# A two-layer decoder on one core: the units of four chains laid in a new order on every engine

## The reference, cut to what matters

```python
x = _layernorm(x + _L0_attn_ref(x, ...))         # selective scan (16 states, 512 channels), conv, gate
x = _layernorm(x + _L0_xattn_ref(x, ctx_768, ...))  # cosine similarities of x and a context
x = _layernorm(x + _L0_ffn_ref(x, ...))          # top 2 of 4 experts, 1024 hidden
x = _layernorm(x + _L1_attn_ref(x, ...))         # 16 heads of 64, softmax over 256 keys
x = _layernorm(x + _L1_xattn_ref(x, ctx_768, ...))  # softmax attention to the context
x = _layernorm(x + _L1_ffn_ref(x, ...))          # state c: batch b needs the state after batch b-1
...
def step(h, inp):                 # of the scan: for each channel and state, along the 256 tokens
    dAt, dBxt, Ct = inp
    h = dAt * h + dBxt
    y = jnp.einsum('bdn,bn->bd', h, Ct)
    return (h, y)
```

## Time and profile before

| | |
|---|---|
| time, median of 3 runs | 1320.05 us (1315.18 to 1323.99) |
| profiled execution, first to last instruction | 1318.1 us |
| mean granted TensorE clock (1 is 2.4 GHz) | 0.953 |
| busy: PE / DVE / ACT / POOL | 1170.0 / 1038.5 / 792.2 / 199.2 us |
| instructions | 16965 |

### The profile page before, as it was taken

One profiled execution on the slowest core, in us unless ns is written; L12 is line 12 of the kernel. 1 busy time (PEld: TensorE's weight loads), 2 busy tenths in 40 slices (PEclk: granted clock), 3 DMA queues, 4 the chain that ended last, 5 costly groups with the idle time before them and its releaser, 6 DMA issues.

```text
span 1318.1 us, 16965 instructions
## 1 busy us (share of the span) xinstructions
PE 1170.0 (89%) x6026; PEld 905.1 (69%) x6026; DVE 1038.5 (79%) x1642; ACT 792.2 (60%) x1978; POOL 199.2 (15%) x258
## 2 busy tenths in 40 slices
PE   5786778988988999999998999999999899999984
PEld 3554545766867767877787777877776767677763
DVE  3999799899878997999869998897959994434215
ACT  4334545378637874686657864875577545646624
POOL 0100020111322212121212121111111211010002
PEclk7888879989999999999999999999999989999998
DMA  5611010223231343233322333322232311000211
GB/s 212 205 44 47 34 54 19 72 63 79 37 96 33 84 86 100 53 65 64 81 72 61 66 56 96 82 51 41 63 87 65 80 33 45 1 1 9 64 63 64
DMA packets 41190, 86.67 MB, mean 66 GB/s; under 512 B 3737, under 2 KB 14970, under 8 KB 40466
## 3 DMA queue, kind: packets, MB, share of 16 engines
q1 hardware_dynamic: 27282, 60.42, 14.4%
q0 software_dynamic: 13824, 25.17, 11.0%
HBM read 54.38 MB, written 6.04 MB: 46 GB/s over the span
## 4 chain that ended last, share of the span: by engine, by line
PE 55%; DVE 25%; ACT 10%; issue 5%; DMA 2%; POOL 2%; ACTq 0%; DVEq 0%; SPq 0%; POOLq 0%
PE bank L295 18%; DVE scans L555 7%; PE bank L510 5%; PE bank L1194 5%; PE bank L1174 4%; DVE scans L560 4%; DVE scans L551 3%; PE bank L906 3%; PE bank L1225 3%; PE bank L900 3%; PE bank L712 3%; ACT scans L531 2%; PE bank L1183 2%; DMA scans<-scans 2%; DVE conv L433 2%
## 5 line engine op out<-in xcount | busy, mean ns | idle before, releaser
L555 DVE TENSOR_TENSOR_SCAN scans<-scans 128x1024 f32<-128x1024 f32 x128 | 292.4, 2284 | 15.3 <-ACT scans L531 8.0
L531 ACT ACTIVATE scans<-dt,a_neg 128x255 f32<-128x255 f32 x512 | 220.7, 502 | 0.0
L510 PE MATMUL bank<-scans,ident 128*128 128x256 f32 x640 | 180.7, 418 | 29.1 <-DVE scans L560 20.2
L510 PEld LDWEIGHTS bank<-scans,ident 128*128 128x128 f32 x640 | 125.0, 206 | 67.2 <-DVE scans L560 26.3
L588 POOL DMA_DIRECT2D scans<-scans x96 | 84.5, 880 | 512.4 <-DVE scans L560 512.2
L560 DVE TENSOR_TENSOR scans<-scans,BC 128x1024 f32<-128x1024 f32 x128 | 155.8, 1217 | 1.3
L551 DVE TENSOR_TENSOR scans<-conv,BC 128x1024 f32<-128x1024 f32 x128 | 155.5, 1215 | 0.1
L1194 PEld LDWEIGHTS bank<-v,ya 128*128 128x128 f32 x1024 | 122.6, 192 | 21.5 <-issue 20.4
L1194 PE MATMUL bank<-v,ya 128*128 128x65 f32 x1024 | 128.5, 276 | 1.8 <-ACT yo L1257 1.6
L1265 ACT ACTIVATE ya<-bank,nmax 128x256 f32<-128x256 f32 x256 | 100.7, 482 | 43.7 <-DVE nmax L1332 43.5
L1332 DVE TENSOR_REDUCE nmax<-bank 128x2 f32<-128x512 f32 x128 | 82.0, 682 | 45.2 <-PE bank L1174 44.8
(11 more groups left out here) (264 smaller groups left out, 2063.8 us busy)
## 6 DMA issues: line engine op xcount, KB each, us to landing
BC<-xpj_scratch SPq DMA_DIRECT2D x31, 1024.0 KB, 5.9
scans<-scans POOLq DMA_DIRECT2D x96, 256.0 KB, 3.3
xin<-in_x SPq DMA_DIRECT2D x8, 256.0 KB, 2.8
conv<-in_x SPq DMA_DIRECT2D x8, 256.0 KB, 2.8
out<-scans SPq DMA_DIRECT2D x8, 256.0 KB, 2.1
kept_x<-x SPq DMA_DIRECT2D x7, 256.0 KB, 2.0
kept_w<-wa SPq DMA_DIRECT2D x7, 256.0 KB, 2.0
BC<-kept_w SPq DMA_DIRECT2D x1, 1792.0 KB, 9.8
```

Source lines behind the costliest of these rows:

```text
L510: last = pe.matmul(sums_of(c), ident[:, :], step_of(b, u)[:, i, :], start=False, stop=(h == UH - 1 and i == SUMMED[b] - 1), skip_group_che ...
L531: ins = act.activation(step[:, j, 1:S], dt[b % 2][:, c, 1:S], ACT.Exp, scale=a_neg[:, c, n:n + 1])
L555: dve.tensor_tensor_scan(flat(H[:, :, :]), flat(H[:, :, :]), flat(dBx), 0.0, ALU.mult, ALU.add).then_inc(s["a_scan"], 1)
```

## The change: another `ORDER`

The five strings are replaced; every letter occurs as often as before, and no function is touched. The same instructions run with the same waits, in another order on each engine. Of the strings, the lines below are those from which places are counted in the text (a line holds 110 letters; PE's eighth line begins at place 770).

```diff
     "pe": (
-        "FFFFFFFWWWSSFFSSYYYFSYFYSYWYSYSYYYSYYSYYSYSFSSFSFSFFSSSFSFWWSWFSWSFSSWFSFWWSWFSWSWWSWWWSWWFSWFSWWWWSWWSWSWSSYS"
-        "YYYYYYYWWYYWYSYWYYYYSYYYYYWFYSYYYYWYYYYWYWSYYYSYYYYYWYYWSYYYWWYFSYWFYYYWYFSSYWWFYYWSYYWWYYSYYYYSWWWSWWFFSYYYYY"
...
-        "WWYWYFWYYYSYYWYYYSYYWYWWSYYYYWYYWWYWWYYWSWWSYWYWWSWWWWWSYYYYYSYWYWSSYYSYWYWSYWYYYSYWYWYYSWYWYWWWWWWSYSYSWSYYYY"
-        "YYWWYYWYYYWYYWYYYYYYYWYWWYYWYWWYWWYWYWWYYYWYWWYYYYYWWYYWYYWYYWYYYYYWWYYYYYYYWYYWYYWYYWWYYWYYYYYWYYYYYWYYYYYWYY"
-        "YYYWYYYYYWYYYYYWYYYYYWYYYYYYYYYYWWWWWWWWWWWWWWWWWWWWWWW"
+        "FFFFFFFFSFSSWWWFSFSYYFSSFFFSSYYSYFWYYYSYSYYYSYSSYYSSSSYWFFWWFSSWSWFSFFSFWWWSSSWWWSFWWFSWWSWWWWWWSWWWSSYSYYYWSY"
+        "YYYYYSYSSYYYWSWYYYYWYYSYWYYWYSYYYYYYYSYWYYWYYWYYFYYSYYSYYYYYWSWYYWYYSWYWYWYWYWYSWYWYYWWSWYYSWFWSFWFSYSYYYYWSWY"
...
+        "WYYWSYYWFYYYSYYWYYWYYYWSYYYWWYWYSWWYWYYWWSWYYWWSYWYWWSYYWYWYSYYYYWSYWSWYWYYYWYYWYSWYYWYWYSWWYSYWWYSYWYYWYYYSYY"
+        "YSWYYSYYSYYYYYWWWYYYWYWYYYYYYWYWYWYYWYWWYWWYYWYWWYWYYWWYWWYWWWYYYYYWWYYYYYWYYYYWYWYYYWWYYWYWYYYYWYYYYWYWYWYYYY"
+        "WYYYYWYYYYYYYYYWYYWYYYYYYYYYYYYYYYWWWWWWWWWWWWWWWWWWWWW"
     ),
     "act": (
-        "FFFFFFFFFSSSSSSFSSFFSSSSFFSSFSSWSSSSSSSSSSSSFFSSFSSFFFFFFSSSSSSSWFSSWFFSSFSSWFSSSSFSSFWWSSWFSSWSSWWSSWFWSSWFSS"
...
+        "FFFFFFFFFSSSFSSFFSSSFFSSSFSFSFFSSSFSFFSSSSWSSSSSSSSFSSSFSSSSFSWFWFSFSSFWSSFSFFSSFWSSWWSSWWSSSWFSFSWSWSSWSWWSWS"
...
     ),
     "dve": (
-        "FWWFFFFFSSWWSSWWSFSSWSFSSFSYSSYSYSSYSYSSYSYSSYSYSSYSYSSYSYSSYSYSSYSFSSSFSSFSFSSSSSSFSFSFFSSSSSSSSFSSSFSSFSFSSW"
-        "SSSSSSWSFSSFSWSSWSWSSFSFSSWSWSSSSSWSSSSWSSSSSSWSSWSSSSYYSYSSYSYSSYYSWFYYSSYSWYYYSSFYYSYWSSWYYSYWSYYSYFSFSSYYYS"
...
+        "FFFFFWWFSSSSFSSSFSWSSFSWSWSWSFSSWSFSSFSFSSYSYSSFSYSSFSYSSYSYSSYYSYSSYSYSSSYSSSSSSYSSFYSFSSYYSSSSFSSSFSWFSSFSWS"
+        "SFSFSSSFSSWSWSSWSFSSWSWSSSSSWSSSSWSSSSSWSWSSSSSYSYSYSYSYSSSYYSSSYYSSSYWSYYSYWYYSYFSYYSYSWSYSYSWYSYYSSWYSYYSSFY"
...
```

More of the change, by code:

```diff
@@ L64 @@
[L64 to L68, removed]
@@ L69 @@
-        "YWYYYYYWYYYYYWWYWWWWWWWWWWWWWWWWWWWWW"
+        "FFFFFFFFFSSSFSSFFSSSFFSSSFSFSFFSSSFSFFSSSSWSSSSSSSSFSSSFSSSSFSWFWFSFSSFWSSFSFFSSFWSSWWSSWWSSSWFSFSWSWSSWSWWSWS"
+        "SSSWYSWSYYYYYYYSSSYYSYYSSWYYSWYSYYWSYYSYYFYYYSYYWYWYYSYYYYSYWYYSFYYSYYYFYSWSWSYYWYFYYSSWYWYYWSSSYWYWSSSWSYFSSF"
+        "WSYSSWYFWYWWSWYYWYWWFWYWSSSFWYSSYYWSSWWYYSSFSYWSYWFYYWYYYWSYYYSFYYSYYWYYWYYSSYYSYSWYYYYYYYSYYFSFWSWYWYSWYYYWSS"
+        "WSYWWYSWSSYYSYSWSWSWYYFWWWSWYWYYWWFYWSSSYYSWSSSYWYYWYYWSSFYYSYYYSWWSYYSYWYYSFSYYWYYYSSYYWYYWYWYFYYYSWSYFWYWSYY"
@@ new lines @@
+        "YYWSFYWWYSSYWYYSSWFYWSYFFYSYFYSSSWWSWFSYWWYSWWWWYYYWYWFYWSSSYSSSYWSWYYWSYYSFYYWYWSYYWSYYFYYWYSSYYFYSYYSFYYWYYY"
+        "WSSWYYYYYWWFYWSYWYYYSWYYFYYWYWSSWFSYSYYWSYYSSSSFWSWWYYWWFSWWSSYYSWWYYWYWWYWYWYYWYYSSSSSYSYWYYWYFSWYYSYYYFWSYYY"
+        "SYSYWYWYYSYSYWYYSYYSWWYWYYYYYSYYWSYYWYWSYWSWYWSSFYYYSSWWSWFSYWWYWSFSWWYWYYYSSWFYWFSSSYWYYFWYYSYWWYFYYYFYYYSSSS"
+        "YWYSWYFWYSYSWSYYYFYYWYYYWYSYSSWYYYYWSYWWYYSWSYWSYWSYWYYYWSSWYSSYYYSYSSWWWSSYWWYSWWYSYWYWWYSWSSSYWYYYSYSYWYWYYW"
+        "YYYYYYYYYYYYYSWYWYWYYYWYYYYYWWYWYYYYWWYWYWYYYWWYWYYWYWYWWWYYYWYWYWYYWYYWWYYYYWYYWYYYYYYYWWYYYYYYYYYWWYYYYYYYWY"
@@ new lines @@
+        "SFSFSSSFSSWSWSSWSFSSWSWSSSSSWSSSSWSSSSSWSWSSSSSYSYSYSYSYSSSYYSSSYYSSSYWSYYSYWYYSYFSYYSYSWSYSYSWYSYYSSWYSYYSSFY"
+        "SWSSWYSFSSWSWSSFSYSSSYSSSWSSWSWSSYSYSSSYSFSYWFWFSWFSSSYSSSYYSWSSWSYSSYSSSYYSWYSFSYYYWSYYSYSYFSWYYSSYWSYYSYSWSY"
+        "SSYYWSWSSFSYSWSWFSSSSSSWSWSWYSYSSSSYSYWSWYWSYSFSSYSWSSSYYSSSWYSSYSFYSSYYSSSYSYWYSSFYWYYSYFSYWSYWWYSSSYYSYWWSSY"
+        "SYFSYWSSWSSYFSFFWSSWSSWSYSYSSSFSYSSYWSSYWWYSFSSSWYSSSSYYWSSSSYYSFYSFYSYYSWSSYYSYWYYSYFYSWYWSYWSYSSWYSWYSSYYSYW"
+        "SFSWSFYSSSFSSWWSWSYSSYSSSSYSYSWYWSYWSYSSSFSWYWSYSSYSYYSSSYSSYFSWYSSYYWYSYYSYSWSYYWWSSYYSYFWYSSWYYSFYSSSYSWWSSS"
@@ L80 @@
+        "WSSWSSWYSYSSSSSFYYWSYWSSWSYSSYFSYSYSSFSSFYYSWYFYYSSYWSSSSYYSWYSFSWYYSYSFYYSWSYWWYSSYSYWSSWYYSSSWSYWSSSYSSWSSSW"
+        "SWSYSYSSSSYYSSWSYWWYSSYSSSYYSSSSSYYSYWWYYYSSYYSYYYWYYYWYYYWYWWYYWYWWYWWWYWYYYYYYWYWYWYYYYYYYYWYYYWYYYYWYYYYYYY"
         "YYWWWWWWWWWWWW"
```

26 lines of the change are left out of this document (9 added, 17 removed).

## The result

The new order is slower: median 1344.43 us of four runs (1334.19 to 1347.14) beside 1320.4 us of the kernel before, ratio 1.0167 with a 95% interval of 1.0121 to 1.0212. That is some 22 us by the ratio, 26.4 us in the profiled execution (1344.5 for 1318.1). It lies above the range I gave, and on the other side of my forecast of 1312.

What follows compares the result with a forecast made beforehand. DVE was taken to bound 30 to 250 us, PE 356 to 1175, then a chain. 1318.1 - 6.6 - 2.7 + 0 + 1.7 = 1310.5 us, plus 1.95 from profile to median: 1312, range 1297 to 1331.

Steps and rivals of the forecast that it cites:

- The start: 30 to 142 us: four DVE waits go, so S0's end comes 6.6 us earlier; bounds 0 and 10.5.
- S1 beside x0: 142 to 250 us: rope units of Y0 fill DVE's waits at S1's end, 2.7 us gained; bounds 0 and 5.
- if Y1 starts as late as now: A stated test at the start of Y1: the prediction is wrong if Y1 starts no earlier than before.
- The body: 356 to 1175 us: PE's 49.7 us of idle time taken as unchanged, 0; bounds 27 less and 17 more.
- the 15 us that I gave myself: A stated test: wrong if PE's idle time from Y0's to Y6's end differs by over 15 us from 49.7.
- POOL and SP: POOL's folds and SP's loads move with their scans; costed at nothing, as the ring of three buffers hides them.
- The tail: From 1175 us, Y7 and z7: three edits on PE sum to 1.7 us later; bounds 1 earlier and 5 later.
- 2 x 3.1 us: Y7's two open pairs: the tail's added length by the skill's clock rule if they fell to 1.2 GHz; not counted.
- late sums at the end of the scan: Slower rival: PE's last sum of S7 comes 11 us later and the end slips, 1333 us; chance 0.13.
- Given back at Y1: Rival: Y1 starts as now, the lead is lost and only the tail's 1.7 us are left, 1322 us; chance 0.15.
- The body that closes up: Rival: PE's idle share in the body falls from 6.1% to 4.45%, 1299 us; chance 0.27.
- the rule on the share of weight loads: Skill's measure of TensorE's fullness: PE at 69%, more room in the body, first rival's sum or less.

Runs made afterwards that it cites:

- old_to_S1: Old strings up to the end of S1, the new ones for all that is left; median 1335.0 us, ratio 1.0097 to the kernel before.
- S0_only: The kernel before with the new strings up to the end of S0 only, old ones behind; median 1329.8 us, ratio 1.0082.
- body_but_Y4: The kernel before with new strings from Y0's end to Y6's end, except the stage of Y4, left old; median 1320.2 us, ratio 1.0005.
- after_sp_old: The kernel after with SP's old string alone (38 of its 89 places differ); 1360.3 us, ratio 1.0271 to the kernel before.
- tail_only: The kernel before with old strings up to Y6's end and the new strings behind; median 1325.9 us, ratio 1.0044.
- tail_fill: Old strings to Y6's end and new tail, with z7's w_vo product moved into the pause of Y7's last pair; 1322.0 us, ratio 0.9986.
- delay2: The kernel before with DVE's product for S0's last piece done three times instead of once, 2.4 us more of DVE; 1320.8 us, ratio 0.9996.

## Why the prediction was wrong

The parts add up: start 9 us (after less old_to_S1), body 8, tail 6, together 23, where the ratio of the whole gives 22. I had -9.3, 0 and +1.7.

- **The start, -6.6: wrong in sign.** The step that failed is to count four waits as time saved without looking for what comes next on the same engine. The front of batch 1, which I had liked early because its tanh is then ready, now stands between the exponentials of S0 on ACT, waits there for PE (6.17 and 2.57 us), and DVE's scan waits 4.10 us at 90.50; the gate at S0's end waits 2.53 us. S0's first residual came at 139.59, not 132.6; in the profiles with the old strings up to there it stands between 135.1 and 140.8. I had given 0 as the bound on that side "if for each wait that goes another comes". The new wait that I feared for the copy to w_qk is in no row. S0_only measured +11, and its profile has as much: 1.7 us of lateness, 5.9 by products at the half level ahead of Y0's end, which I had not priced, and 3.4 in the body that I have not followed.
- **S1 beside x0, -2.7 with S1's end as now: wrong.** The 10 us of rope units ahead of S1's end were counted rightly; the 9.3 us that were to pay for them didn't come. S1's end was 12 us late, and Y1 started no earlier than before (its first unit on ACT at 372.69 for 369.82). My own test, "if Y1 starts as late as now", failed here. Y0's end at 343 came to 359.61.
- **The body, 0: wrong, 19.2 us in the profile, some 9 of it by the runs handed over from the start.** PE's idle time there is 55.9 us for 49.7, well within the 15 us that I gave myself; that test passed and was the wrong one. 12.9 us are PE's busy time at a clock of 0.97 for 0.99 with nine products more. The mean of stages said nothing of the stage in which most of the loss fell.
- **POOL and SP, costed at nothing: the step that failed in the body, as far as the runs show it.** I named the ring of three buffers as the cover. The cover was the work of DVE and PE laid between a scan's last product and its gate, and the new order took it away: 11.8 us of DVE's waiting, 5.8 of PE's, and body_but_Y4 without that stage lost nothing. Without the transfer the stage is 3.7 to 5.3 us shorter; the cause of the 8.5 us left in it stays open. Nor was SP's order free: its old string under the other new ones cost 14 us in after_sp_old.
- **The tail, +1.7, measured +4.9 in the profile and +6 by tail_only.** The mechanism was right in the main: pairs with ACT in the chain (three for two, the last one among them), and the recurrent products at once behind Y7, without the 0.2 us that I had estimated. That all lines of Y7's pairs are PE's in the old order was misread: ACT's copy stands in one of them (1206.40, 0.61 us). The mis-sized term is the clock. I set it at nothing because 0.95 stood in that stage of the old order; measured, the three groups that end Y7 take some 5 us longer at the half level (3.66 for 1.85, 9.21 for 7.17, and 4.46 for 3.18 with the output transposes and their copies), and tail_fill shows it. The Trainium skill (TensorE: Matmul & The Clock Gate, Part 1) says that idle time lets the clock fall; the trace agrees, 0.53 in the 12 us behind the pause and 1.00 with the pause filled. I had weighed that and dropped it. That its price in the prediction, 2 x 3.1 us, is near the 6.1 us of the profile and the 7.7 of the runs is luck: it put the half level into the two open pairs, whose products ran at full speed (1.13 and 1.94 us), and it fell on the products behind the last pair.
- **The rivals.** The slower one, late sums at the end of the scan at 1333, was nearest in time and not in cause: S7's end was 29 us late with everything else. "Given back at Y1" happened, and behind it came what no rival had. The body that closes up, and the rule on the share of weight loads that the prediction set beside it, are borne out by no run: they ask for 21 us, and the best order found is 10 us faster.

## What to carry to other kernels

When an order is changed, follow for each wait on a transfer the units that stand between issue and use on every waiting engine, and compare their number and time before and after: that cover is what a reordering spends without showing it. Look at the last work ahead of a serial end for pauses of PE, since the products behind them can run at half clock, and put a product that is free to move into the pause. Cut a reordering into stretches and run each alone before taking all of it: here one stretch of the slower kernel beat the kernel before.

## What the hardware showed that I had not expected

- Time and mean granted clock move together from run to run of one program: the 29 runs of the kernel before beside S0_only lie between 1312 us (at 0.962) and 1329 (at 0.948), and between the two groups of delay2 0.011 of mean clock goes with 7.6 us.
- A pause of PE of 1.7 us in Y7's last pair (tail_only) was followed by products at half the full speed, 0.53 in the next 12 us and 0.69 over 22; with one product of 2 us laid into it the same stretch was at 1.00.
- A 256 KB accumulate of POOL that lands in 3.3 us by the median took 10.4 us beside two 1 MB loads of SP. The slowest in the kernel before takes 10.5, and there PE waits 8.5 us for all 96 of them together, 21.7 in the kernel after: the cover decides, not the transfer's time alone.
